# A four-layer conv and attention kernel: the experts' matmuls of batches 0 to 5 on gathered token blocks

## The reference, cut to what matters

```python
router_logits = jnp.einsum('bsd,ed->bse', X, Wr) + br
router_weights = jax.nn.softmax(router_logits, axis=-1)
top_k_weights, top_k_indices = jax.lax.top_k(router_weights, TOP_K)      # TOP_K = 2
expert_outputs = jnp.einsum('bsd,ehd->bseh', X, We) + be                 # 8 experts, 256 x 256
gathered = jnp.take_along_axis(expert_outputs, top_k_indices[..., None], axis=2)
combined = jnp.sum(top_k_weights[..., None] * gathered, axis=2)
out = jnp.einsum('bsd,hd->bsh', combined, Wo) + bo
```

## Time and profile before

| | us |
|---|---|
| median of 3 runs | 654.12 (652.51 to 654.73) |
| the profiled execution | 654.19 |
| its span, first to last instruction | 652.4 |
| TensorE busy | 570.7 (87%) |
| VectorE busy | 475.4 (73%) |
| ScalarE busy | 300.3 (46%) |
| GpSimd busy | 118.6 (18%) |
| mean granted clock of TensorE | 0.97 |

### The profile page before, as it was taken

How to read it: one execution, slowest core, us unless ns; L and a number is a source line. 1 busy time by engine, 2 the same in 40 slices (tenths; PEclk the granted TensorE clock), 3 DMA queues, 4 the chain that set the end, 5 groups by cost and what they waited for, 6 DMA issues and landing times.

```text
span 652.4 us, 10840 instructions
## 1 busy us (share of the span) xinstructions
PE 570.7 (87%) x3994; PEld 385.1 (59%) x4032; DVE 475.4 (73%) x1273; ACT 300.3 (46%) x472; POOL 118.6 (18%) x115
## 2 busy tenths in 40 slices
PE   9884776867989989989889888999999999999897
PEld 4743433745766756757667666656575756565443
DVE  4677868857678687787876776786968778786664
ACT  2346677626555455554545554243343425253110
POOL 2121000351313313313223132103030200000000
PEclk9886899889999999999999998999999999999999
DMA  9600000574135043143143240405032140000000
GB/s 335 258 1 1 1 0 2 127 220 128 52 98 150 28 123 114 56 132 113 35 146 89 59 146 19 127 1 162 2 100 62 41 122 16 2 17 1 17 18 16
DMA packets 40636, 51.15 MB, mean 78 GB/s; under 512 B 4180, under 2 KB 33620, under 8 KB 40276
## 3 DMA queue, kind: packets, MB, share of 16 engines
q1 hardware_dynamic: 40584, 50.46, 25.8%
HBM read 35.63 MB, written 14.68 MB: 77 GB/s over the span
## 4 chain that ended last, share of the span: by engine, by line
PE 50%; DVE 24%; issue 3%; DMA 1%; SPq 1%; ACT 1%; POOL 1%; DVEq 0%; ACTq 0%
PE ps L1317 13%; PE ps L1204 8%; PE ps L1196 7%; DVE nmax L1466 7%; PE ps L1279 4%; PE ps L1267 3%; PE ps L1247 3%; DVE xn L1422 2%; PE ps L1263 2%; PE ps L1188 2%; DVE stats L1411 2%; DVE acc L1551 2%; PE ps L1286 2%; PE ps L1242 2%; PE ps L1239 1%
## 5 line engine op out<-in xcount | busy, mean ns | idle before, releaser
L1466 DVE TENSOR_REDUCE nmax<-ps 128x2 f32<-128x512 f32 (+1 forms) x192 | 130.5, 681 | 70.5 <-PE ps L1247 67.7
L1368 ACT ACTIVATE PT<-ps 128x512 f32<-128x512 f32 x192 | 114.0, 597 | 145.3 <-PE ps L1267 143.2
L1317 PE MATMUL ps<-wm,xnT 128*128 128x512 f32 x256 | 120.1, 600 | 0.0
L1362 ACT ACTIVATE QS<-ps 8x1024 bf16<-8x1024 f32 x64 | 65.0, 1016 | 31.3 <-PE ps L1252 30.1
L1267 PE MATMUL ps<-QS,KS 110*128 110x256 bf16 (+3 forms) x512 | 75.0, 248 | 0.0
L1551 DVE SCALAR_TENSOR_TENSOR acc<-ps,gate,acc 128x256 f32<-128x256 f32 x128 | 61.6, 481 | 16.5 <-PE ps L1317 14.2
L1317 PEld LDWEIGHTS ps<-wm,xnT 128*128 128x128 f32 x256 | 44.6, 190 | 38.3 <-issue 38.0
L1263 PE MATMUL ps<-fixb 128*128 128x256 bf16 (+1 forms) x192 | 60.2, 314 | 7.5 <-DVE nmax L1466 3.5
L1148 POOL TENSOR_TENSOR rstd<-ve,fix 128x2 f32<-128x2 f32 x31 | 21.5, 693 | 247.9 <-DVE ve L1417 247.9
L1196 PE MATMUL ps<-xnT,by_dim 128*128 128x256 f32 x256 | 62.6, 390 | 2.2 <-ACT xnT L1333 2.2
L1168 POOL TENSOR_TENSOR parts<-rest,fix 128x512 bf16<-128x512 f32 x30 | 38.0, 1268 | 139.1 <-DVE rest L1435 100.5
(11 more groups left out here) (217 smaller groups left out, 882.8 us busy)
## 6 DMA issues: line engine op xcount, KB each, us to landing
parts_dram<-parts SPq DMA_DIRECT2D x32, 384.0 KB, 3.1
QS<-parts_dram SPq DMA_DIRECT2D x96, 128.0 KB
KS<-parts_dram SPq DMA_DIRECT2D x96, 128.0 KB, 2.6
wt<-wt_dram SPq DMA_DIRECT2D x1, 2562.0 KB, 19.2
wm<-wm_dram SPq DMA_DIRECT2D x1, 2449.0 KB, 13.0
xc<-x_dram SPq DMA_DIRECT2D x8, 256.0 KB, 5.3
out_dram<-res SPq DMA_DIRECT2D x8, 256.0 KB, 2.1
w<-w_dram SPq DMA_DIRECT2D x1, 845.0 KB, 7.5
```

The costliest lines, as they stand in the source:

```text
L1317: mm = pe.matmul(d, normT(stage, batch)[:, c, t * P:(t + 1) * P], M("We", c * EXPERTS * CH + e * 2 * CH, 2 * CH), start=(c == 0), stop=(c ...
L1362: act.activation(QS[MAX_AT:MAX_AT + MAX_ROWS, stack(stage, batch), 4 * n:4 * n + 4, :], bank(piece)[MAX_AT:MAX_AT + MAX_ROWS, 0:PIX].unsqu ...
L1368: act.activation(PT[:, pt_slot(piece, n), :], bank(piece), ACT.Exp).then_inc(drain(piece), 1)
L1466: dve.tensor_reduce(group[:, 0, :] if part == 0 else group[:, 1, 2 * part - 2:2 * part], bank(piece).rearrange("p (j n) -> p j n", n=w_), ...
```

## The change

The tokens of batches 0 to 5 no longer meet all 8 experts. They are sent in two **waves**, batches 0 to 3 and batches 4 and 5, through a region of memory for each wave (`by_expert0_dram`, `by_expert1_dram`) that holds the rows sorted by expert. Batches 6 and 7 keep the pieces `E` as they were (`DENSE_AT`). For a sent batch there are these new pieces:

- `RK` (PE): the rank of each token within each expert, by small bf16 matmuls of the 0/1 masks of the top two with a triangle and with ones; `SL` (DVE) makes row numbers of it (`slots`). `RT` 3 gets some more small operations (masks, running sums, `gains`).
- `SC` (POOL): four indirect transfers write the rows of `xn` to their places. The next batch's `LNb`, which writes `xn` anew, waits for them (`rows_sent`).
- `BL` (DVE, on the last batch of a wave): the list of blocks of 128 rows, each of one expert: its row (`block_row`) and its expert's place in the weights (`block_expert`). The number of blocks is fixed: 24 in wave 0, 16 in wave 1, worked as 12 and 8 **pairs**.
- For each pair: `BD` (SP loads two row numbers to registers and issues two loads of 128x256), `BT` (PE: 4 transposes; ACT copies them to `by_dim`), `BY` (PE loads the expert's place to a register for each block and multiplies by those weights; ACT copies to `rows_out`), `BS` (SP stores the two blocks back in place).
- `GA` (POOL: four indirect transfers fetch a batch's two rows per token, after the last pairs of the wave are stored), `CB` (DVE: four weighted additions), and `CT` as before.

The pairs of wave 0 stand at steps 170, 172, ... 192, those of wave 1 at steps 194 to 201; the gathers follow at steps 196 to 199 and 204, 205. The sum of a batch now lies in the residual `X` itself, in place of `acc`. At the start SP fills both regions with zeros (14.68 MB) from the cleared tile `hp2`, and DVE waits for that (`rows_zeroed`) before it writes to `hp2`.

```diff
+WAVES = ((0, 1, 2, 3), (4, 5))
+FIRST_PAIR = (38, 38)
+PAIR_STEP = (2, 1)
+PAIRS_IN, PAIRS_TURNED, PAIRS_OUT = 3, 2, 2
+def pairs(wave):
+    blocks = (2 * room(wave) + EXPERTS * (P - 1)) // P
+    return (blocks + 1) // 2
...
-        ("GB", 3, 0, 32), ("E", 3, 0, 35), ("E", 3, 1, 36), ("E", 3, 2, 37), ("E", 3, 3, 38), ("E", 3, 4, 39),
-        ("E", 3, 5, 40), ("E", 3, 6, 41), ("E", 3, 7, 42), ("CT", 3, 0, 44)),
+        ("GB", 3, 0, 32)),
+DENSE_AT = {6: range(35, 43), 7: range(35, 43)}
...
+    out += [("RK", 3, 0, 31), ("SL", 3, 0, 32), ("SC", 3, 0, 32)]
+    start, apart = FIRST_PAIR[wave], PAIR_STEP[wave]
+    end = start + apart * pairs(wave) + 2
+    if batch == last:
+        out.append(("BL", 3, 0, 32))
+        for k in range(pairs(wave)):
+            at = start + apart * k
+            out += [("BD", 3, k, at - 3), ("BT", 3, k, at), ("BY", 3, k, at + 1), ("BS", 3, k, at + 1)]
+    at = end + BODY * (last - batch) + (batch - WAVES[wave][0])
+    out += [("GA", 3, 0, at), ("CB", 3, 0, at + 1), ("CT", 3, 0, at + 2)]
...
+                sp.wait_ge(padded_zero, 2)
+                sp.wait_ge(wt_loaded, 16)
+                zeros = hp2[:].rearrange("p b h w -> p (b h w)")[:, 0:8 * CH].bitcast(F32)
+                for w, rows in enumerate(by_expert):
+                    sp.dma_start(rows.rearrange("(p a r) n -> p a (r n)", p=P, r=4),
+                                 zeros.unsqueeze(1).broadcast_to([P, all_rows(w) // P // 4, 4 * CH])).then_inc(rows_zeroed, 16)
...
+                    if k == 2:
+                        dve.wait_ge(rows_zeroed, 16 * len(WAVES))
...
+                if kind == "SC":
+                    wait(pool, "slots_ready", ("SL", stage, batch, 0))
+                    for k in range(2):
+                        for t in range(2):
+                            pool.indirect_dma_start(by_expert[wave_of(batch)][:, :],
+                                                    bass.IndirectOffsetOnAxis(slots[:, batch, k, t:t + 1], 0),
+                                                    xn[:, 1, t, :], None).then_inc(sems["rows_sent"], 16)
...
+                if kind == "BT":
+                    wait(pe, f"block_loaded{pair_at(piece, PAIRS_IN)}", ("BD", stage, batch, n))
+                    src = rows_in[:, pair_at(piece, PAIRS_IN)]
+                    for j in range(2):
+                        for c in range(NC2):
+                            mm = pe.transpose(d[:, (j * NC2 + c) * P:(j * NC2 + c + 1) * P], src[:, j, c * P:(c + 1) * P],
+                                              F("ident"))
+                if kind == "BY":
+                    w = wave_of(batch)
+                    drained(pe, ("BT", stage, batch, n))
+                    wait(pe, "blocks_ready", ("BL", stage, batch, 0))
+                    for j in range(2):
+                        k = 2 * n + j
+                        at = pe.value_load(block_expert[0:1, w, k:k + 1], min_val=0, max_val=(EXPERTS - 1) * CH)
+                        for c in range(NC2):
+                            weights = M("We", c * EXPERTS * CH, EXPERTS * CH)
+                            mm = pe.matmul(d[:, j * CH:(j + 1) * CH], turned_in[:, pair_at(piece, PAIRS_TURNED), j, c, :],
+                                           weights[:, bass.ds(at, CH)], start=(c == 0), stop=(c == 1))
...
+                if kind == "BY":
+                    full(act, piece)
+                    if pair_before(piece, PAIRS_OUT):
+                        wait(act, f"block_stored{pair_at(piece, PAIRS_OUT)}", ("BS", *pair_before(piece, PAIRS_OUT)))
+                    copy_out(flat(rows_out[:, pair_at(piece, PAIRS_OUT)]))
...
+                    if stage == 3 and 0 < batch <= SENT:
+                        wait(dve, "rows_sent", ("SC", stage, batch - 1, 0))
...
+                if kind == "CB":
+                    wait(dve, f"rows_fetched{par}", ("GA", stage, batch, 0))
+                    for k in range(2):
+                        for t in range(2):
+                            into = X[:, 2 * batch + t, :]
+                            op = dve.scalar_tensor_tensor(into, fetched[:, par, t, k, :], gains[:, batch, k, t:t + 1], into,
+                                                          ALU.mult, ALU.add)
```

More of the change, by code:

```diff
@@ L8 @@
 I32 = mybir.dt.int32
+U32 = mybir.dt.uint32
 ALU = mybir.AluOpType
@@ L77, with wave_of, room, all_rows @@
 TURN_BACK = (7, 6)
+WAVES = ((0, 1, 2, 3), (4, 5))
+SENT = sum(len(w) for w in WAVES)
+FIRST_PAIR = (38, 38)
+PAIR_STEP = (2, 1)
+PAIRS_IN, PAIRS_TURNED, PAIRS_OUT = 3, 2, 2
+def wave_of(batch):
+    return next(k for k, w in enumerate(WAVES) if batch in w)
+def room(wave):
+    return len(WAVES[wave]) * PIX
+def all_rows(wave):
+    return EXPERTS * room(wave) + EXPERTS * P
+def pairs(wave):
+    blocks = (2 * room(wave) + EXPERTS * (P - 1)) // P
+    return (blocks + 1) // 2
 PARTS_OF_MAX = 2
@@ L126, with dense, flow @@
         ("RT", 3, 1, 28), ("RT", 3, 2, 29), ("RT", 3, 3, 30), ("GT", 3, 0, 31),
[2 rows of a table removed]
-}
[1 row of a table added]
+}
+DENSE_AT = {6: range(35, 43), 7: range(35, 43)}
+def dense(batch):
+    at = DENSE_AT[batch]
+    return tuple(("E", 3, n, at[n]) for n in range(EXPERTS)) + (("CT", 3, 0, at[-1] + 2),)
+def flow(stage, batch):
+    if stage == 0 or batch >= SENT:
+        return FLOW[stage] + (dense(batch) if stage else ())
+    wave = wave_of(batch)
+    out, last = list(FLOW[stage]), WAVES[wave][-1]
+    out += [("RK", 3, 0, 31), ("SL", 3, 0, 32), ("SC", 3, 0, 32)]
[8 more added lines that the diff above has]
+    out += [("GA", 3, 0, at), ("CB", 3, 0, at + 1), ("CT", 3, 0, at + 2)]
+    return tuple(out)
 AHEAD = {1: 6, 2: 12}
@@ L1145, in pool_piece @@
                 kind, stage, batch, n = piece
+                par = batch % 2
                 if kind == "LNa":
```

206 lines of the change are left out of this document (187 added, 19 removed).

## The result

The changed kernel takes 680.33 us (median of 4 runs, 679.24 to 681.15) against 653.32 for the kernel before: a ratio of 1.0418, 95% interval 1.0377 to 1.0459, so 27 us more. Forecast were 670 us, +16; the range of 638 to 698 holds the time. The profiled execution has a span of 679.2 us, 26.8 more than before.

What follows compares the result with a forecast made beforehand. Dense-expert bodies were taken as PE bound, router bodies without experts as set by a chain of waits. Bodies -20.0, pairs stretch +4.7, start +1.3, pair waits +20.0, tail +10.0 gave +16.0 us: 670, range 638 to 698.

Steps and rivals of the forecast that it cites:

- the sum: All terms added: -20.0 + 4.7 + 1.3 + 20.0 + 10.0 = +16.0 us, giving 670 us.
- A: Three bodies from 399.90 to 512.88, losing 24 expert pieces: 31.0 us each, a gain of 20.0 us.
- B: From 512.88 to the dense batches' return: pairs replace expert pieces, plus moved transposes and block list; +4.7 us.
- D: PE's new waits in pairs, for ScalarE's copy (0.4 us) and register loads (0.6 us): 20 pairs, +20.0 us.
- E: Tail: last pair's stores, wave 1's gathers and additions delay the last batch's router; +10 us.
- C: Start and first router: zero fill hidden, fills and pads 0.5 us, router step of batch 0 0.8; +1.3 us.
- A's worst end: Bodies with a second 2.7 us wait and the slot list on the path: 34.7 us each, a gain of 9.
- the 29.20 row: Profiled body with router and without experts, 29.20 us, taken as base for the three bodies' forecast of 31.0.
- fourth rival: Clock falls to half speed after each pair's stall, for 43.4 us of pairs: +43, 713 us; chance 0.03.
- the rule of the Trainium skill: PE idling between bursts starts each at the low clock; by it the pairs' stalls would slow what follows.

Runs made afterwards that it cites:

- The run with own rows: Changed kernel with scatters two steps later, behind the SPLITs, and a separate buffer of normalized rows for odd batches; 679.79 us, 1.0399 to the kernel before.
- all four changes: Changed kernel with odd-batch norm rows and late scatters, earlier wave 0 block loads, later block matmuls, later additions and final transposes in both waves; 659.64 us.
- the run with the expert known: Changed kernel with a fixed expert's weights for each block and no register load on TensorE; 679.48 us, 1.0410 to the kernel before.

## Why the prediction was right, and what in it was not

**Right:** slower, and by the named places: what PE is relieved of in the bodies is smaller than its work, and pairs' waits and tail are larger than the rest. The tail is the best of it: forecast +10 from 19 us of stores, gathers and additions ahead of the last router, measured +11.0, and 8.0 come back when only the additions and final transposes move. From the end of the last block matmul to the last batch's router it takes 19.4 us (630.55 to 649.94), forecast 19.0. The zero fill is hidden; up to the bodies the sum had +1.3 and the trace -1.2. A gather takes 1.26 us from issue to issue, forecast 1.2. The sum fell 10.7 us short: 8.5 in A, 3.7 in B and D, 1.0 in E, less 2.5 in C.

**A was too good by 8.5 us.** Forecast 31.0 a body, measured 33.8. Of the 2.8, 2.2 are the wait behind DVE operations held by the `SPLIT`s; the rest lies probably in matmuls at the lower clock (0.85 to 0.90). A's worst end had a second wait of 2.7 us, but as a repetition of the wait for `xn`, not at this place. The prediction named the queue that the scatters enter, but priced it only for the scatters' own landing and the next norm's power; what else moves on POOL, and on what it then lies, wasn't asked. The run with own rows, 31.9 a body, comes within 0.9 us of the forecast and bears out the 29.20 row as the base.

**B and D were right in sum, 24.7 against 28.4, with wrong parts.** Of 20 us of pair waits 10.0 are in the trace, and the step that failed is the register load: taken at 0.6 us a pair, 12 us, it shows 4.3 us of waits and a stretch longer by 7.1 where it stands, of which 0.9 reach the whole, and 3.3 with all four changes, neither clear of the noise. The waits for the copy were sized better, 5.7 against 8. It is wrong to multiply a wait by twenty when another engine's work, here 20 us of gathers, sets the end of the same stretch. The floor of 600 ns that the Trainium skill, "DMA: Bandwidth & Descriptors", section "Latency and other measured facts", gives for such a load doesn't show here: the trace has 0.30 us (0.29 to 0.64), with all its address arithmetic about 0.5. In place of the missing 10 us stand two things that the sum didn't have: the first rows' wait of 5.2 us behind SP's twelve stack loads with the slow stretch behind it, 6.0 by experiment, and the stretch up to the first pair, for which the sum held -4.0 (three expert pieces less, block list) and the trace +2.9; one more held cast, 1.20 us, and PE's wait of 1.4 us behind it lie there. 24.7 - 10 + 6.0 + 6.9 = 27.6 of the 28.4. Of these terms the 6.0 was tried by a run; the others are readings of one trace. That the wrong parts so nearly cancel is luck.

**The clock.** The prediction's fourth rival had it fall after each pair's stall of 1 us; it doesn't: it is 1.00 from 537 to 630, where PE waits eleven times at pairs, up to 1.7 us, and is busy between. It is 0.85 in the bodies with waits of 2.7 and 2.2 us, 0.80 behind the 5.2 us wait for the first rows, 0.87 in the tail with its wait of 5.7 us. So what the prediction says of the rule of the Trainium skill ("TensorE: Matmul & The Clock Gate", section "HAM oscillation — how this bites in real kernels"), that the trace is against it for waits of about 1 us and with it for 2.7, holds in the changed kernel. The kernel that this section of the Trainium skill tells of idles longer between its bursts than 1 us, so it didn't speak for the fourth rival as the prediction has it. The longest single wait doesn't decide alone, though: in the run with the expert known, waits of 1.3 and 1.6 us that end at 617.94 and 622.39 are followed by 0.50 from 624 on. The sum had such a wait only as A's worst end, and some 20 us more of PE's work than before are lost to the low clock; how much of that is on the path wasn't taken apart.

## What to carry to other kernels

Before work is taken off the engine that bounds, look at what that engine does next: here it waited, ran at half speed behind the waits, and 39 us of relief became 12.7. A step put into an in-order queue moves everything behind it, and the price lies where that lands: on another engine's small operations, on loads, on the next norm. A gain at one wait can go into the next: 7.1 us of register loads taken away brought 0.9. So changes that bring nothing alone may do so together; here the joint run gave half as much again as the single gains, but it holds an edit that was never run alone.
